# A sum of two tiles goes from VectorE to GpSimd, and half of the weight preparation moves behind the first projection

## The reference

```python
x = emb[inp]                                  # 8000 x 256 table, gathered by token
q, k, v = x @ Wq.T + bq, x @ Wk.T + bk, x @ Wv.T + bv        # 16 heads of 16
h = softmax(q k.T / 4) v @ Wo.T + bo          # attention over the 128 tokens
# gated state of the normalized h
Bu_proj = layernorm(h) @ B_w.T @ C_w.T
state = exclusive_scan(decay = sigmoid(log_decay), Bu_proj)  # along the tokens
h = h + sigmoid(layernorm(h) @ gate_w.T + gate_b) * state
h = h + layernorm(h) @ sign(ffn_weight).T
```

## Time and profile before

| | |
|---|---|
| time, median of 3 runs | 780.36 us (780.24 to 781.73) |
| the profiled execution | 785.06 us |
| its span | 782.9 us |
| TensorE busy | 703.9 us, 90% |
| VectorE busy | 579.0 us, 74% |
| ScalarE busy | 576.9 us, 74% |
| GpSimd busy | 205.1 us, 26% |

### The profile page before, as it was taken

How to read it: one execution, slowest core, us unless ns; L and a number is a source line. 1 busy time by engine, 2 the same in 40 slices (tenths; PEclk the granted TensorE clock), 3 DMA queues, 4 the chain that set the end, 5 groups by cost and what they waited for, 6 DMA issues and landing times.

```text
span 782.9 us, 21221 instructions
## 1 busy us (share of the span) xinstructions
PE 703.9 (90%) x7047; PEld 650.6 (83%) x7047; DVE 579.0 (74%) x1307; ACT 576.9 (74%) x1643; POOL 205.1 (26%) x271
## 2 busy tenths in 40 slices
PE   1379899999999999999999999999999999999864
PEld 0268889888899899989889899989999899989753
DVE  4345688777777887777777887777787888778663
ACT  2178787787888787788788788788888788788610
POOL 7200132133222332233222332233222332221121
PEclk9889999999999999999999999999999999999985
DMA  5232222333333223333333222333333222332000
GB/s 136 94 95 82 68 78 76 95 109 108 96 107 95 71 78 90 107 107 107 94 107 95 72 80 88 107 107 107 94 107 103 71 75 86 107 108 95 15 14 27
DMA packets 56015, 69.67 MB, mean 89 GB/s; under 512 B 6768, under 2 KB 41648, under 8 KB 55984
## 3 DMA queue, kind: packets, MB, share of 16 engines
q1 hardware_dynamic: 52048, 60.48, 24.2%
q0 software_dynamic: 3072, 8.39, 5.7%
q10 hardware_dynamic: 864, 0.40, 0.2%
HBM read 10.52 MB, written 8.39 MB: 24 GB/s over the span
## 4 chain that ended last, share of the span: by engine, by line
PE 45%; DVE 15%; SPq 11%; DMA 11%; issue 9%; ACT 7%; POOL 1%; DVEq 1%; ACTq 0%; another core or an unknown queue 0%; POOLq 0%
PE ps_g L635 23%; DMA q_stack<-q_low 9%; SPq L237 8%; PE ps_t L707 7%; PE ps_s L635 5%; PE ps_c L635 4%; PE ps_g L684 3%; SPq L242 3%; DVE neg_max L497 3%; ACT k_high L399 3%; DVE xn L530 2%; DVE gated L589 2%; PE ps_g L733 2%; DVE v_aug L578 2%; ACT probs L353 2%
## 5 line engine op out<-in xcount | busy, mean ns | idle before, releaser
L353 ACT ACTIVATE probs<-ps_s,neg_max 128x128 f32<-128x128 f32 x1024 | 298.1, 397 | 99.1 <-DVE neg_max L497 99.1
L497 DVE TENSOR_REDUCE neg_max<-ps_s 128x4 f32<-128x512 f32 x256 | 176.2, 688 | 144.4 <-PE ps_s L635 135.9
L362 ACT COPY probsT<-ps_t 128x512 f32<-128x512 f32 x256 | 156.2, 610 | 31.2 <-PE ps_t L707 29.5
L707 PE MATMUL ps_t<-ident,probs 128*128 128x128 f32 x1024 | 156.0, 275 | 5.3 <-ACT probsT L362 5.1
L635 PE MATMUL ps_s<-k_stack,q_stack 128*128 128x256 f32 x512 | 125.6, 327 | 14.4 <-DMA q_stack<-q_low 13.6
L707 PEld LDWEIGHTS ps_t<-ident,probs 128*128 128x128 f32 x1024 | 119.3, 141 | 14.2 <-issue 4.5
L635 PEld LDWEIGHTS ps_s<-k_stack,q_stack 128*128 128x128 f32 x512 | 78.4, 194 | 20.7 <-DMA q_stack<-q_low 20.0
L292 POOL TENSOR_TENSOR state_high<-state_in,ones_col 128x512 fp32r<-128x512 f32 x32 | 33.2, 1036 | 199.1 <-DVE state_in L624 199.1
L305 POOL TENSOR_TENSOR rs<-ve,neg_half 128x2 f32<-128x2 f32 x32 | 22.1, 692 | 217.9 <-DVE ve L524 217.9
L283 POOL DMA_INDIRECT x_emb<-in_emb,id_col x64 | 64.9, 1014 | 36.3 <-PE ps_g L684 20.4
L635 PE MATMUL ps_c<-probsT,v_aug 128*32 128x128 f32 x2048 | 69.3, 276 | 0.0
(11 more groups left out here) (126 smaller groups left out, 1866.7 us busy)
## 6 DMA issues: line engine op xcount, KB each, us to landing
k_stack<-k_high SPq DMA_DIRECT2D x128, 128.0 KB
q_stack<-q_high SPq DMA_DIRECT2D x64, 256.0 KB
k_stack<-k_low SPq DMA_DIRECT2D x64, 128.0 KB
q_stack<-q_low SPq DMA_DIRECT2D x32, 256.0 KB
out<-y SPq DMA_DIRECT2D x32, 256.0 KB, 2.1
x_emb<-in_emb,id_col POOLq DMA_INDIRECT x64, 4.3
raw<-in_wkT SPq DMA_DIRECT2D x1, 256.0 KB, 3.1
raw<-in_wqT SPq DMA_DIRECT2D x1, 256.0 KB, 4.1
```

The costliest lines, as they stand in the source:

```text
L353: last = nc.scalar.activation(probs[s % 2][:, j], ps_s[s % 2][:, j * SEQ:j * SEQ + SEQ], ACT.Exp, bias=neg_max[s % 2][:, j:j + 1])
L362: nc.scalar.copy(probsT[st][:], ps_t[:]).then_inc(act_pT, 1)
L497: nc.vector.tensor_reduce(neg_max[s % 2][:], ps_s[s % 2][:].rearrange("p (h k) -> p h k", h=HPS), axis=AX.X, op=ALU.max, negate=True).then ...
L707: last = nc.tensor.transpose(ps_t[:, j * SEQ:j * SEQ + SEQ], probs[st % 2][:, j], ident[:])
```

## The change

There are two edits. First, the sum h1 = gated + h0 is taken from VectorE's turn and put into GpSimd's, between the copies of token ids and rs2; its semaphore is now GpSimd's. Second, ahead of the turns only wk, wq, wv and the scaled bias of the queries are prepared. The other preparations (wg, wo, ws, wf_sign, powers, the gate's bias) become a function `prepare` that ScalarE and VectorE run at the head of turn 0, after they have issued pair 0's key and query parts in turn -1; TensorE transposes the powers at the head of turn 0 (`turn_powers`) and waits for the rest at the head of turn 1 (`await_prepared`). The product B_w C_w goes to the bank ps_c, as g3 is used by turn -1.

```diff
-        def turns(eng, turn):
+        def turns(eng, turn, ahead=()):
             for t in range(-2, 6):
+                for at, prepare in ahead:
+                    if t == at:
+                        prepare()
                 turn(t, t % 2)
@@ gpsimd, turn
                 copy_ids(t + 2, par)
                 if exists(t - 3):
+                    await_event(pool, dve_gated, 1, t - 3, 1)
+                    await_event(pool, dve_y, 1, t - 4, 1)
+                    nc.gpsimd.tensor_tensor(h1[:], gated[:], h0[1 - par][:], ALU.add).then_inc(pool_h1, 1)
+                if exists(t - 3):
                     await_event(pool, dve_ve2, 1, t - 3, 1)
@@ scalar
-            act.wait_ge(small_loaded, 96)
-            nc.scalar.activation(e_ld[:], ld_col[:], ACT.Exp, scale=-1.0).then_inc(exp_ld, 1)
-            nc.scalar.mul(bq_col[:], bq_raw[:], SCALE).then_inc(act_prep, 1)
-            nc.scalar.copy(gb_high[:], gb_row[:]).then_inc(act_prep, 1)
-            nc.scalar.copy(gb_parts[0:64], gb_row[0:64]).then_inc(act_prep, 1)
-            act.wait_ge(act_prep, 3)
...
-            act.wait_ge(raw_loaded[0], 32)
-            high_part(wg[0], raw[0])
-            act.wait_ge(raw_loaded[2], 32)
-            high_part(wo[0], raw[2])
-            act.wait_ge(wstate_mm, 1)
-            high_part(ws[0], g3)
+            act.wait_ge(small_loaded, 96)
+            nc.scalar.mul(bq_col[:], bq_raw[:], SCALE).then_inc(act_prep, 1)
+            act.wait_ge(act_prep, 1)
+
+            def prepare():
+                nc.scalar.activation(e_ld[:], ld_col[:], ACT.Exp, scale=-1.0).then_inc(exp_ld, 1)
+                act.wait_ge(raw_loaded[0], 32)
+                high_part(wg[0], raw[0])
+                act.wait_ge(raw_loaded[2], 32)
+                high_part(wo[0], raw[2])
+                act.wait_ge(wstate_mm, 1)
+                high_part(ws[0], ps_c)
+                nc.scalar.copy(gb_high[:], gb_row[:]).then_inc(act_prep, 1)
+                nc.scalar.copy(gb_parts[0:64], gb_row[0:64]).then_inc(act_prep, 1)
...
-            turns(act, turn)
+            turns(act, turn, ((0, prepare),))
@@ vector
             low_part(wv, raw[2][:], 3)
-            low_part(wg, raw[0][:], 4)
-            low_part(wo, raw[2][:], 5)
-            low_part(ws, g3[:].rearrange("p (c o) -> p c o", c=C), 6)
...
+            dve.wait_ge(act_prep, 1)
+
+            def prepare():
+                dve.wait_ge(exp_ld, 1)
+                nc.vector.tensor_scalar(e_ld1[:], e_ld[:], 1.0, None, ALU.add).then_inc(prep_step, 1)
...
+                low_part(wg, raw[0][:], 4)
+                low_part(wo, raw[2][:], 5)
+                low_part(ws, ps_c[:].rearrange("p (c o) -> p c o", c=C), 6)
...
+                nc.vector.tensor_scalar(raw[0][:], raw[1][:], 0.0, None, ALU.is_lt).then_inc(prep_step, 1)
...
+                dve.wait_ge(powers_turned, 1)
+                nc.vector.tensor_copy(powers_tok[:], ps_t[:, 0:D]).then_inc(powers_made, 1)
+                dve.wait_ge(powers_made, 3)
@@ vector, turn
-                if exists(t - 3):
-                    await_event(dve, dve_gated, 1, t - 3, 1)
-                    await_event(dve, dve_y, 1, t - 4, 1)
-                    nc.vector.tensor_tensor(h1[:], gated[:], h0[1 - par][:], ALU.add).then_inc(dve_h1, 1)
 
                 maxima(3)
                 context_norm(1, g2)
                 if exists(t - 3):
-                    norm_stats(t - 3, h1, dve_h1, stats2, dve_st2)
+                    norm_stats(t - 3, h1, pool_h1, stats2, dve_st2)
@@ tensor
             for c in range(C):
-                last = mm(g3[:, c * D:c * D + D], bw_sb[:, c * P:c * P + P], cw_sb[:])
+                last = mm(ps_c[:, c * D:c * D + D], bw_sb[:, c * P:c * P + P], cw_sb[:])
             last.then_inc(wstate_mm, 1)
             pe.wait_ge(ids_ready, 1)
-            pe.wait_ge(w_low, 6)
-            pe.wait_ge(prep_done, 1)
...
+            pe.wait_ge(w_low, 3)
+
+            def turn_powers():
+                pe.wait_ge(powers_made, 2)
+                for c in range(C):
+                    last = nc.tensor.transpose(ps_t[:, c * P:c * P + P], powers[:, c], ident[:])
+                last.then_inc(powers_turned, 1)
+
+            def await_prepared():
+                pe.wait_ge(w_low, 6)
+                pe.wait_ge(prep_done, 1)
+                pe.wait_ge(powers_made, 3)
+                pe.wait_ge(bias_made, 3)
+                pe.wait_ge(bias_step, 4)
+                pe.wait_ge(act_prep, 3)
...
-            turns(pe, turn)
+            turns(pe, turn, ((0, turn_powers), (1, await_prepared)))
```

More of the change, by code:

```diff
@@ L163, in build @@
                                                       sem("dve_xn1"))
[L164 removed]
+        pool_h1, dve_st2, dve_mv2, dve_ve2, dve_xn2 = (sem("pool_h1"), sem("dve_st2"), sem("dve_mv2"), sem("dve_ve2"),
                                                       sem("dve_xn2"))
@@ L486, in _ @@
-            dve.wait_ge(powers_turned, 1)
-            nc.vector.tensor_copy(powers_tok[:], ps_t[:, 0:D]).then_inc(powers_made, 1)
-            dve.wait_ge(powers_made, 3)
+            dve.wait_ge(act_prep, 1)
+            def prepare():
+                dve.wait_ge(exp_ld, 1)
+                nc.vector.tensor_scalar(e_ld1[:], e_ld[:], 1.0, None, ALU.add).then_inc(prep_step, 1)
+                dve.wait_ge(prep_step, 7)
+                nc.vector.reciprocal(decay[:], e_ld1[:]).then_inc(prep_step, 1)
+                dve.wait_ge(prep_step, 8)
+                for c in range(C):
+                    nc.vector.tensor_tensor_scan(powers[:, c, 1:SEQ], decay[:, c:c + 1].to_broadcast([P, SEQ - 1]),
+                                                 zero_col[:].to_broadcast([P, SEQ - 1]), powers[:, c, 0:1],
+                                                 ALU.mult, ALU.add).then_inc(powers_made, 1)
+                low_part(wg, raw[0][:], 4)
+                low_part(wo, raw[2][:], 5)
+                low_part(ws, ps_c[:].rearrange("p (c o) -> p c o", c=C), 6)
+                dve.wait_ge(raw_loaded[1], 32)
+                dve.wait_ge(w_low, 4)
+                nc.vector.tensor_scalar(raw[0][:], raw[1][:], 0.0, None, ALU.is_lt).then_inc(prep_step, 1)
+                dve.wait_ge(prep_step, 9)
+                nc.vector.scalar_tensor_tensor(wf_sign[:], raw[1][:], 0.0, raw[0][:], ALU.is_gt,
+                                               ALU.subtract).then_inc(prep_done, 1)
+                dve.wait_ge(small_loaded, 96)
+                dve.wait_ge(act_prep, 2)
+                nc.vector.memset(one_of_each[:].bitcast(fp32), 0.0).then_inc(bias_step, 1)
+                dve.wait_ge(bias_step, 1)
+                for row in (0, 64):
+                    nc.vector.memset(one_of_each[row:row + 1].bitcast(fp32), 1.0).then_inc(bias_step, 1)
+                nc.vector.tensor_tensor(gb_parts[64:P], gb_row[64:P], gb_high[64:P].bitcast(fp32),
+                                        ALU.subtract).then_inc(bias_step, 1)
+                dve.wait_ge(powers_turned, 1)
+                nc.vector.tensor_copy(powers_tok[:], ps_t[:, 0:D]).then_inc(powers_made, 1)
+                dve.wait_ge(powers_made, 3)
@@ L627, in turn @@
                 low_features(t - 3, xn2T, g3, act_xn2T, pe_ffn, dve_xn2lo)
-            turns(dve, turn)
+            turns(dve, turn, ((0, prepare),))
         @block.tensor
```

## The result

The changed kernel takes 756.59 us (median of 4 runs, 755.29 to 758.06) against 780.48 (4 runs, 780.24 to 781.73): ratio 0.9692, 95% interval 0.9674 to 0.9709. The forecast was 755.1, range 750 to 767. Its profiled execution took 756.35 us, span 754.5.

The account below looks back on a forecast made before the run. It took a nearly empty 25.27 us start, then turns bound by the copies' loop through VectorE and TensorE's own way; start -13.7, turns -12.9, end +1.3 sum to -25.3, from 780.36 to 755.1 us, range 750 to 767.

Parts of the forecast that it names:

- The start: Before the turns: transposes of pair 0's embeddings move from 25.27 to 11.6 us, worth -13.7 us (ends -14.6 and -13.1).
- the rival of the reloads: At the start: reloads of raw delay pair 0's gathers, part of the shortened-start case, 758 to 766 us; chance 0.09.
- the chain from transposes to scores: At the start: projection and copies from pair 0's transposes to first scores, assumed unchanged in length, keeping the 13.7 us.
- The cover: Start: VectorE's 5.7 us of moved work fits its 5.91 us of idle time before maxima(0), so nothing is added.
- The steady turns: Turns with h1 and copies: 21.6 us instead of 22.06, 0.46 over 28 turns, -12.9 us (ends 0 and 18.5).
- the loop of copies: Steady turn: cycle from scores(0) through VectorE and stack copies to the next scores(0), 22.14 us becoming 21.53.
- TensorE's floor: Steady turn: TensorE's own way without its 0.4 us wait for k_low, 21.76 - 0.4 = 21.4 us.
- My base of 22.06: Steady turns before the change: average over 27 turns, from pair 4's start to pair 31's, 22.06 us each.
- The end: Last pairs: h1 stands on the chain, +0.62 us for pairs 30 and 31, 0.1 for 29; +1.3 (0 to 2.5).
- The sum: Whole kernel: -13.7 - 12.9 + 1.3 = -25.3 us; profiled 785.06 to 759.8, median 780.36 to 755.1.
- The rivals: Whole kernel: only the start pays (0.20), the start pays less (0.09), slower (0.03), the change does nothing (0.03).
- The slower one: Steady turns: h1 slow on GpSimd, loss beginning at 2.5 us for h1, 795.4 us at 3 us; chance 0.03.

Follow-up runs that it names:

- gather_wait: The changed kernel, with GpSimd in turn 0 waiting for pair 0's copies to land before issuing pair 2's gathers; 755.40 us, ratio 0.9670.
- cmp_tt: The kernel before, with the comparison over raw written with a second tensor instead of a constant; 781.67 us against 781.70.
- prep_only: The changed kernel with h1 back on VectorE, so only the preparation edit remains; 770.90 us, ratio 0.9858 to the kernel before.
- both_tt: The kernel before, with the comparison over raw and e_ld + 1 both written with a second tensor instead of a constant; 778.95 us, ratio 0.9934.
- the second trace of before: The kernel before, unchanged, run and profiled once more; median 783.26 us of 12 runs, span 780.9.
- h1_twice: The changed kernel, with the same 128x512 sum first computed into a spare tile so h1 is later; 795.76 us, ratio 1.0193 to the kernel before.
- gather_early: The kernel before, with each turn's gathers issued on GpSimd some 7 us earlier, behind a tiny GpSimd operation; 775.92 us, ratio 0.9918.

## Why the prediction was right, point by point

**The start** was forecast at -13.7. Pair 0's transposes moved by 13.2, and 10.4 of it were left by pair 3. Three things lie between.
- 0.5: the second gather was issued at 7.64 instead of 7.26, because the first one took 1.59 us to issue instead of 1.20; in the seven traces with the early preparation it was 1.58 to 1.60 six times and 1.37 once, in the seven others 1.20. It ran while VectorE made the low part of wk (5.58 to 6.27 in the changed kernel), which before came more than 4 us later. That this is the reason was not tried, and one row speaks against it: before the change a gather ran beside such an instruction (13.99, with the low part of wg from 14.23) and took its usual 0.98. The rest of the 0.5, 0.14, passed between the landing and the first transpose. The landing itself took 4.29 us, as forecast, but by luck: I had taken the median of all gathers, and this one took 3.43 before. In all seven traces with the early preparation it took 4.1 to 4.8 us, in the seven others 3.4 to 3.7, and the reloads of raw are now issued beside it (6.30, 7.30, 9.07). So the rival of the reloads seems to have taken place in a small way, by about 0.7 us; no run isolates it.
- 1.7: the landing of pair 0's last copy, 4.09 instead of 2.46 us. GpSimd's second zeroing holds the gathers for pair 2 until 22.40, and they fall among the copies (18.6 to 24.5); before, they were issued at 27.16, ahead of them. This is the step of the sum that failed: I let the chain from transposes to scores keep its length because TensorE's, ScalarE's and SyncE's parts of it did, and I had not asked what GpSimd would issue beside it. gather_wait shows it: with the gathers held back the landing is 2.46 again.
- 1.1: in the next turn the landing was 3.52 us instead of 2.51, which is nearly all of it, and TensorE's granted clock was at its lower level (1.2 GHz, share 0.50) longer than in the kernel before:

```profile
50.50:52.50 2.00, 2.00 (x11) 2.00 (x11) 1.28 (x3) 1.48 (x5) 0.00 (x0) 0.50 0.00 0
```

  This is a window after. In the trace before, the window from 62 to 64, 3 us behind the same scores, was at 0.92 again. TensorE had been idle longer ahead of them in the changed kernel (3.52 against 2.51 us of landing), but that this lengthens the lower level is not shown: in cmp_tt the window from 57.3 to 64.2 was at 0.51 too, behind a landing of 2.51.

  That landing was 3.57 in gather_wait and 3.60 in prep_only too, with no gather beside it. The traces show one thing that may be the reason. In the changed kernel a packet of the queue that the profile calls instruction stands among these copies, 1.6 us behind the issue of the last one (window 44 to 48.5):

```profile
q14 instruction: 1, 0.01, 0.4%
```

  It stands there, 1.5 to 1.7 us behind the issue, in all eight traces in which the landing took 3.5 to 3.6 us (those with the early preparation, and both_tt), and 4.3 to 4.8 us behind it, when the copies had landed, in the six with 2.5 us. No run tested it, so the cause stays open.

**The cover** held. VectorE's moved work ended at 27.5 and maxima(0) began at 28.89, after 1.37 us of idle time instead of none: the scores were the later ones. That room came from the late landing. In gather_wait, where the copies land on time, maxima(0) starts at 27.41, directly behind the moved work, so the cover is as tight as it was forecast to be. The comparison took 0.55 us (forecast 0.69), and e_ld + 1 was held until the zeroing ended at 21.88 (20.06 + 1.82). That is what the rule of the Trainium skill, "SBUF — State Buffer", practical consequences, had let expect; it was a little less than forecast, because e_ld + 1 began later:

```profile
21.30 0.61 DVE L470 TENSOR_SCALAR e_ld<-e_ld 128x2 f32<-128x2 f32 x1
...
24.70 0.55 DVE L485 TENSOR_SCALAR raw<-raw 128x512 f32<-128x512 f32 x1
...
28.89 1.29 DVE L508 TENSOR_REDUCE neg_max<-ps_s 128x4 f32<-128x512 f32 x2 [1.37 <-PE ps_s L642]
```

**The steady turns** were forecast at 21.6 instead of 22.06, -12.9. That the gain needs k_low brought forward as well as the copies is shown by the experiments; the size was too small. From pair 9 on the turns alternate between 21.34 and 21.51 us and scatter no more, because TensorE arrives later than the stacks in every one of them: the loop of copies, which I had at 21.53 and which set my 21.6, no longer binds. TensorE's floor came out at my 21.4, but partly by luck: I had its busy time at 21.3 and the wait for k_low gone, and it is 21.23 with 0.13 of the wait and 0.06 of shorter idle times left. My base of 22.06 also mixed long first turns with settled ones of 21.94, where the copies hardly bound any more. And the first turns with h1, where landings of 5 us and more stood in the kernel before, gained more than the rest. From pair 3 to pair 31 it was 17.4 us. h1's 1.28 us were 1.30, the wait of VectorE 0.24 instead of 0.11: the handover to GpSimd is 0.13 us here (gated ends at 419.81, h1 starts at 419.94) instead of the 0.07 that I took from the last turns.

**The end** was forecast at +1.3, and the rows at the place bear it out: from gated's start to the statistics' start the changed kernel takes 0.1 us more for pair 29 and 0.6 more for each of pairs 30 and 31. The length of the whole end can't show it, as it differs by 3 us between two traces of the kernel before: it is +1.4 against the second trace of before, and a gain of 1.6 against the first.

**The sum** was -25.3 and the medians differ by 23.9. The start's 3.3 us too many, the steady part's 4.5 too few and the end's 0.1 nearly cancel; by the traces with the second one of before it is -10.4 - 17.4 + 1.4 = -26.4. That the medians give 2.5 less is within what two samples of a kernel that scatters over 7 us allow; the kernel before had medians of 780.5 to 783.3 in its samples. The sum against the profiled execution (759.8) came out 3.4 above what was measured (756.35), for the base was a long execution.

**The rivals.** None took place as priced. The slower one had the right mechanism and a wrong point: I had the loss begin at 2.5 us for h1, and the runs put it at about 2.2. I let the start and the end keep 12.4 us whatever h1 takes. But the start left only 10.4, and the end grows with h1 (from pair 31's embeddings to the end of the span 82.1 us in the changed kernel, 88.7 in h1_twice).

## What to carry to other kernels

When two cycles of nearly equal length hold a loop, look for the edit that shortens both, and check it with one that shortens only one of them; here the latter was worth 0.1 to 0.25 us a turn and the former 0.5. Read in the settled turns which wait is there each time: the chain of one turn can name the other. A start-up chain that is moved forward keeps its length only if what runs beside it moves too: list what the other queues will issue in the new place. And before work goes to a slower engine in a loop, work out how late its result may be; here 0.9 us more would have used up the whole change.

## What was not expected of the hardware

Two gathers issued by GpSimd among nine copies issued by SyncE lengthen the landing of the last copy from 2.5 us to between 4.1 and 4.6 (gather_wait against the change, gather_early against before), though the DMA engines are busy only a third of the time (share 0.32 in a turn). And a wait for GpSimd's memset is inherited: it holds the next tensor_scalar of VectorE, however small (4.27 us for two elements per partition).
